# Order of units 8 to 11, and the low part of one row sum on another engine

## What is computed

```python
x = x + tanh(g_xattn) * xattn(layernorm(x), ctx, Wq, bq, Wk, bk)
x = x + tanh(g_ffn)   * ffn(layernorm(x), W_up, W_gate, W_down)

# ffn, with every weight replaced by its ternary form q in {-1, 0, 1} times a scale
up, gate = x @ wu.T, x @ wg.T          # 512 -> 2048
hidden   = silu(up) * gate
out      = hidden @ wd.T               # 2048 -> 512
```

## Time and profile before

| | |
|---|---|
| median of three runs | 394.9 us |
| the profiled execution | 395.01 us |
| its span in the trace | 393.2 us |
| granted clock of TensorE | 1.0, full, in all of it |
| TensorE busy | 388.2 us, 99%, 2000 matmuls |
| VectorE busy | 330.2 us, 84% |
| ScalarE busy | 269.8 us, 69% |
| GpSimd busy | 183.9 us, 47% |

### The profile page before, as it was taken

One profiled execution on the slowest core, in us unless ns is written; L12 is line 12 of the kernel. 1 busy time (PEld: TensorE's weight loads), 2 busy tenths in 40 slices (PEclk: granted clock), 3 DMA queues, 4 the chain that ended last, 5 costly groups with the idle time before them and its releaser, 6 DMA issues.

```text
span 393.2 us, 6214 instructions
## 1 busy us (share of the span) xinstructions
PE 388.2 (99%) x2000; PEld 219.3 (56%) x2000; DVE 330.2 (84%) x501; ACT 269.8 (69%) x366; POOL 183.9 (47%) x199
## 2 busy tenths in 40 slices
PE   8999999999999999999999999999999999999997
PEld 6676775554444444444444444556545665656886
DVE  0778897988799975789888979999999989798974
ACT  3887988899777786869897982856287566564400
POOL 0498727767845031403169462643639447261000
DMA  8999977799600030020029470006230000000014
GB/s 287 404 402 407 408 232 184 176 261 183 160 2 0 1 108 0 13 96 0 2 60 190 86 148 2 0 1 214 78 139 0 2 1 2 0 2 1 2 61 154
DMA packets 44048, 43.91 MB, mean 112 GB/s; under 512 B 30833, under 2 KB 33009, under 8 KB 42993
## 3 DMA queue, kind: packets, MB, share of 16 engines
q1 hardware_dynamic: 44016, 43.53, 36.3%
HBM read 29.89 MB, written 6.29 MB: 92 GB/s over the span
## 4 chain that ended last, share of the span: by engine, by line
PE 84%; DVE 6%; ACT 4%; issue 4%; DMA 1%; POOL 1%; DVEq 0%; ACTq 0%; POOLq 0%
PE pair L924 20%; PE pair L926 20%; PE pair L1052 14%; PE pair L1000 8%; PE pair L815 7%; PE pair L838 6%; PE pair L788 4%; PE pair L772 3%; PE pair L799 2%; DVE x_sb L1855 1%; DVE xf L1804 1%; DMA xf<-in_first 1%; PE pair L853 1%; DVE sh L1814 1%; ACT xf L1395 1%
## 5 line engine op out<-in xcount | busy, mean ns | idle before, releaser
L924 PE MATMUL pair<-xb_hi,w_sb 128*128 128x512 f16 x448 | 169.8, 379 | 0.9 <-DVE xf L1799 0.5
L926 PE MATMUL pair<-xb_lo,w_sb 128*128 128x512 f16 x448 | 169.8, 379 | 0.0
L924 PEld LDWEIGHTS pair<-xb_hi,w_sb 128*128 128x128 fp8e4 x448 | 43.8, 98 | 54.0 <-DVE xf L1799 1.3
L926 PEld LDWEIGHTS pair<-xb_lo,w_sb 128*128 128x128 fp8e4 x448 | 43.8, 98 | 49.5 <-issue 0.3
L1344 ACT ACTIVATE xf<-xf,small 128x512 f32<-128x512 f32 x48 | 34.5, 720 | 43.5 <-DVE xf L1799 23.6
L1804 DVE SCALAR_TENSOR_TENSOR xf<-xf,small 128x512 f32<-128x512 f32 x48 | 41.7, 870 | 8.5 <-ACT xf L1344 8.4
L1855 DVE SCALAR_TENSOR_TENSOR x_sb<-pair,small,x_sb 128x256 f32<-128x256 f32 (+1 forms) x85 | 37.4, 472 | 6.3 <-PE pair L1052 5.8
L1000 PE MATMUL pair<-x_sb,sh 128*128 128x512 bf16 x192 | 42.4, 379 | 0.0
L626 POOL TENSOR_TENSOR w_sb<-w_sb 128x512 fp8e4<-128x512 fp8e4 x8 | 8.8, 1101 | 55.1 <-ACT w_sb L1215 55.1
L1000 PEld LDWEIGHTS pair<-x_sb,sh 128*128 128x128 f16 x192 | 18.8, 98 | 22.6 <-DVE x_sb L1839 0.2
L1809 DVE TENSOR_TENSOR sh<-xf,sh 128x512 f16<-128x512 f32 x34 | 30.6, 906 | 0.9 <-ACT sh L1357 0.8
(11 more groups left out here) (207 smaller groups left out, 769.2 us busy)
## 6 DMA issues: line engine op xcount, KB each, us to landing
w_sb<-in_wugT SPq DMA_DIRECT2D x8, 1024.0 KB, 14.9
x_sb<-in_x SPq DMA_DIRECT2D x4, 1024.0 KB, 12.8
xf<-in_wdT SPq DMA_DIRECT2D x4, 1024.0 KB, 7.5
xt_sb<-in_wdT SPq DMA_DIRECT2D x4, 1024.0 KB, 4.9
xt_sb<-in_xT SPq DMA_DIRECT2D x12, 256.0 KB, 5.8
x_dram<-x_sb SPq DMA_DIRECT2D x8, 256.0 KB, 3.5
out<-x_sb SPq DMA_DIRECT2D x8, 256.0 KB, 4.2
x_sb<-x_dram SPq DMA_DIRECT2D x4, 512.0 KB, 3.9
```

The costliest lines, as they stand in the source:

```text
L924: pe.matmul(dst[:, m * 512:(m + 1) * 512], w[:, o:o + P], hi[:, k], start=start and k == 0, stop=False, skip_group_check=not start)
L926: last = pe.matmul(dst[:, m * 512:(m + 1) * 512], w[:, o:o + P], lo[:, k], start=False, stop=k == 1, skip_group_check=not start)
```

## The change

Three engines' queues are written in another order, and one operation changes its engine. No semaphore is new.

- GpSimd makes the low part of S2 for units 6 to 10 and 12 to 14, between the S4 sum (`h_sum_4`) and the low part of S4. In unit 11 VectorE still makes it (and in unit 15, as before). VectorE's calls in units 7 to 11 and 13 to 15 go.
- ScalarE, at the end of unit 7: `copy_5(8)` ahead of `silu(8, "11")`. At the end of unit 8: `shift(1, 0)` and `shift(1, 1)` behind `silu(8, "21")`, not ahead of it. In unit 11: `high_s(10, "S4")` ahead of `silu(11, "12")` and `high_h(11, "11")`.
- VectorE: `low_h(8, "22")` moves from the end of unit 8 behind `make_h(8, "21")` in unit 9. In unit 9 `add_22` goes ahead of `make_h(9, "12")`, and `low_h(9, "11")` goes from behind `add_22` to just ahead of `low_h(9, "22")`.

```diff
@@ GpSimd
             h_sum_4(GB)
+            low_s(GB, "S2")
             low_s(GB, "S4")
@@ GpSimd, units 7 to 14
                 if n == G1 - 1:
                     low_s(n, "S3")
+                if n != G1 - 1:
+                    low_s(n, "S2")
                 low_s(n, "S4")
@@ ScalarE
                 if n == G0:
                     high_h(n, "22")
-                    shift(1, 0)
-                    shift(1, 1)
                     break
...
-                if n == 1:
+                if n in (1, G0 - 1):
                     copy_5(n + 1)
                     silu(n + 1, "11")
...
                 silu(n - 1, "21")
                 if n == G0 + 1:
+                    shift(1, 0)
+                    shift(1, 1)
                     copy_5(n)
@@ ScalarE, unit 11
             high_h(n - 1, "21")
+            high_s(n - 1, "S4")
             silu(n, "12")
             high_h(n, "11")
-            high_s(n - 1, "S4")
             silu(n, "22")
@@ VectorE, unit 7
             evict_half(n, 2)
             evict_half(n, 3)
-            low_s(n - 1, "S2")
             low_t(NU, "B22", xf_half(3, 1))
@@ VectorE, unit 8
             weights_1(2)
-            low_s(n - 1, "S2")
             add_22(n)
...
             low_h(n, "11")
-            low_h(n, "22")
@@ VectorE, unit 9
             make_h(n - 1, "21")
+            low_h(n - 1, "22")
             low_s(n - 1, "S1")
...
             evict_two(n, 3)
-            low_s(n - 1, "S2")
+            add_22(n)
             make_h(n, "12")
-            add_22(n)
-            low_h(n, "11")
             evict_two(n, 7)
             make_h(n, "22")
             evict_two(n, 2)
+            low_h(n, "11")
             low_h(n, "22")
```

## The result

Eight runs each: the kernel before 394.84 us (394.12 to 395.36), the changed kernel 395.93 us (395.47 to 396.71). The ratio is 1.0031, 95% interval 1.0021 to 1.0041: slower by 1.1 us, or 0.3%. The profiled execution after took 396.34 us with a span of 394.2; the one before 395.01 with 393.2.

A forecast was written before the change was run, and what follows sets the result against it. TensorE, busy 99% of the span, was taken to bound the kernel. Terms of 0.94 - 0.30 - 0.35 - 0.63 - 0.24 + 1.82 - 0.41 + 0.42 summed to +1.25, kept as +1.2: 396.1 us, range 393.9 to 397.1.

The forecast's parts named there:

- S2 of unit 6 on GpSimd, +0.94: Unit 7: GpSimd's new row blocks VectorE's low part of S1, delaying evictions and product 1 of unit 8 by 0.94 us.
- Copy ahead of the SiLU, -0.30: Unit 8: product 5's copy runs while ScalarE waited for VectorE, removing the 0.30 us gap ahead of product 3.
- Unit 8, -0.35: VectorE's lighter queue and ScalarE's earlier SiLU bring multiplication 21 forward, removing 0.35 us at unit 9's first final group.
- Unit 9 up to product 4, -0.63 and -0.24: Unit 9: addition of 22 ends earlier, saving 0.63 us ahead of product 4 and 0.24 at the last final group.
- Product 1 of unit 10, +1.82: Behind product 4 of unit 9, three VectorE rows wait for GpSimd, so late evictions delay this product by 1.82 us.
- Unit 10, 0: VectorE loses one low part but only idles, since later additions wait for products or copies: 0, bounds -0.1 and +0.2.
- Unit 11, -0.41 and +0.42: Earlier S4 copy saves 0.41 us ahead of unit 12's product 6; GpSimd's S2 costs 0.42 ahead of unit 11's product 4.
- Units 12 to 14, 0: GpSimd's new row falls into its idle wait and VectorE loses a row in front of idle time: 0.
- the rivals: Whole-kernel alternatives: fast 393.2 us, 12%; only unit 7 costs 394.7, 18%; only unit 9 costs 395.2, 12%; worse 397.1, 8%.
- The fast one: In units 7 and 9 waiting GpSimd rows let VectorE go first; sum -1.5 to -1.9, 393.2 us, 12%.
- a mere sharing of bandwidth: VectorE and GpSimd both run slower; the two blocking terms spread thin and the sum falls to the gaps alone.

The follow-up runs named there:

- experiment 1: Changed kernel with the low part of S2 of unit 6 back on VectorE, behind two evictions of unit 7: 394.98 us, ratio 1.0009.
- experiment 2: Changed kernel with GpSimd's low part of S2 of unit 6 put behind its low part of S4: 394.99 us, ratio 1.0012.
- experiment 5: Changed kernel with every low part of S2 back on VectorE, leaving only the new orders: 395.25 us, ratio 1.002.
- experiment 6: Kernel before with the low part of S2 on GpSimd as in the change, every order kept: 394.75 us, ratio 1.0004.
- experiment 8: Changed kernel, GpSimd's S2 of unit 6 behind S4, unit 9's low h22 in unit 11, unit 10's low S1 behind multiplication 12: 394.15 us, ratio 0.999.
- experiment 4: Changed kernel with GpSimd in unit 9 waiting for the multiplication of 21 before sums S1 and S2: 395.34 us, ratio 1.0017.
- experiment 9: Kernel of experiment 8 with the low part of h22 of unit 9 in unit 10, ahead of the addition of 12: 393.63 us, ratio 0.9975.
- experiment 10: Changed orders with the low part of h22 of unit 9 in unit 10, every low part of S2 on VectorE: 393.76 us, ratio 0.9979.
- experiment 3: Changed kernel with VectorE's low parts of h11 and h22 of unit 9 behind the evictions of part 4: 396.32 us, ratio 1.0044.
- experiment 7: Changed kernel with VectorE's order of before in unit 9 alone, S2 still on GpSimd: 394.92 us, ratio 1.0007.

## Why the prediction was right, point by point

The time (396.1 forecast, 395.9 measured) and the way it comes out of the sum both held. No single term is off by more than 0.13, and those errors nearly cancel, so that the sum is closer than its parts.

1. *S2 of unit 6 on GpSimd, +0.94.* The gap grew from 0.05 to 1.02. VectorE's low part of S1 was forecast at 1.6 and took 1.64. Experiments 1 and 2 show it to be this row, and its place.
2. *Copy ahead of the SiLU, -0.30.* The gap is gone. That does not show that the copy's place did it: TensorE is later against ScalarE by the loss in point 1. In experiments 1 and 5, where that loss is absent, the gap is absent too, and this is the evidence; experiment 6 shows that the loss alone would have closed it too. (In the traces of experiments 1 to 8 a start comes 0.22 us late, the time of one matmul, at the down projection of each of units 3 to 8. These traces hold 1994 matmul records and the others 2000, so at each of the six places one was not recorded, and these count in no sum.)
3. *Unit 8, -0.35.* Gone. Product 6 of unit 9, for whose copy I left 0.1, starts without a gap (250.11). The orders alone close the gap (experiment 5), the move alone leaves 0.12 of it (experiment 6); no run tells the place of the shifts from that of the low part of h22.
4. *Unit 9 up to product 4, -0.63 and -0.24.* Both gaps went wholly, -0.70 and -0.24; the addition ended 0.4 earlier by the clock than I had worked out (258.56 against 258.96), mostly because the profiled execution is 0.2 earlier from before unit 7 (218.26 against 218.46) and the multiplication of "11" was stretched less (1.31 against 1.44).
5. *Product 1 of unit 10, +1.82.* It measured 1.69. The three stretched rows are there, the multiplication 0.58 and the pair of low parts 1.71 longer than alone, where I had 0.64, 0.63 and 1.07. Experiment 4 shows that the pair's meetings with GpSimd's sums are the cause (it leaves the multiplication stretched), and experiment 5 that the order brings them about, not the additional row.
6. *Unit 10, 0.* The gap ahead of product 1 of unit 11 is 0.07, as before.
7. *Unit 11, -0.41 and +0.42.* Now 0 and 0.43. In experiments 8 and 9, with the low part of S1 behind the addition, the 0.43 does not occur, nor in 5 and 10, where S2 stays on VectorE. The gap of 0.41 ahead of product 6 of unit 12 is gone in 5 and 10, with the copy of S4 early and no 0.43 ahead of it, as forecast; it is also gone in experiment 6, where ScalarE has its order of before but TensorE has lost the 0.43, so the changed kernel by itself doesn't tell the two apart.
8. *Units 12 to 14, 0.* A gap of 0.13 came up in unit 12 that I had not.

None of the rivals came true. The fast one, in which a waiting GpSimd row lets VectorE go first, is refuted by both places. (The prediction also calls a mere sharing of bandwidth its fast rival; the condition that it worked out, and that was tested, is this one.) My expectations of the experiments were less good: three came out 0.6 to 2 us slower than I had them (3, 5 and 8), in 3 and 8 because I counted the row that is moved and not what it meets in its new place.

One thing stays open. For the changed kernel and experiments 1 to 7 and 10 the sum of gaps, against 2.13 before, gives the measured difference within 0.5 us. For experiments 8 and 9 it gives -0.8 and -1.4, and the medians say -0.5 and -0.7 (the ratios -0.4 and -1.0). Within the traces nothing is missing: from the last matmul ahead of the first down projection, in unit 3, to the last matmul it is 253.4 us before, 252.6 in experiment 8 and 252.0 in experiment 9, which is the sum of gaps. What comes ahead of that, where nothing was edited, took 135.7 to 137.0 us in the twelve profiled executions. The one of experiment 9 is the shortest of them there, 1.2 below the one before, and so its span is 2.6 shorter and not 1.4. Why its median gained only half of the 1.4 is not shown: there is one trace of each kernel, and single executions differ by more than that.

## What to carry to other kernels

Before a row is moved to GpSimd because that engine is idle, look at which VectorE rows will stand beside it. Against evictions from PSUM it was free; an operation with two SBUF inputs that stood beside a GpSimd row took up to 1.1 us longer, and two low parts in a chain made the 1.7 us gap. In a full queue, putting a waited-for row ahead of others may only hand the wait on, as in experiment 3; find the idle time of that engine in the trace and put the deferrable row there. And when gaps on the bounding engine are small, work out the chain behind the changed place as far as the next thing that is waited for: the gap closed here ahead of product 4 of unit 9 (0.7) was paid for 8 us later (1.7).

## What the runs showed of the hardware

In each meeting looked at the rows' lengths fit strict turns of VectorE and GpSimd. Back to back on both, VectorE's rows of 0.64 took 1.5 to 1.7 each (2.99 for two in the changed kernel and in experiment 5) and GpSimd's of 1.27 took 1.72. Where VectorE's row met only the rest of a GpSimd row, it took 1.1 to 1.4 (1.08 at 249.10 and 1.42 at 266.31 in the changed kernel). An added wait on GpSimd shortened VectorE's same two rows from 2.99 to 1.28 us (experiment 4). VectorE's evictions from PSUM took 0.86 to 0.87 for two with a GpSimd row beside them or not. The granted clock was 1.0 in the kernels before and after and 0.999 to 1.0 in the experiments, so none of this is TensorE's clock.
